# Quantised feed-forward stage: scaled values written as unsigned integers, z quantised on GpSimd

## The reference

```python
def _affine_quantize(x):
    amin, amax = (jnp.min(x), jnp.max(x))
    scale = jnp.maximum((amax - amin) / 255.0, 1e-08)
    zp = jnp.clip(jnp.round(-amin / scale) + QMIN, QMIN, QMAX)
    q = jnp.clip(jnp.round(x / scale) + zp, QMIN, QMAX)
    return (q, scale, zp)
def _qlinear(x, W, b):
    xq, sx, zx = _affine_quantize(x)
    wq, sw = _sym_quantize(W)
    acc = jnp.einsum('bsh,oh->bso', xq - zx, wq)
    return acc * (sx * sw) + b
h = _qlinear(x, W1, b1)
h = jax.nn.gelu(h, approximate=False)
out = _qlinear(h, W2, b2)
```

## Time and profile before

| | us |
|---|---|
| median of 3 runs | 2394.42 (2391.53 to 2396.53) |
| the profiled execution | 2395.65 |
| its span, first to last instruction | 2393.8 |
| the stage that the diff touches | 1087.8 to 1231.2 of it |

### The profile page before, as it was taken

How to read it: one execution, slowest core, us unless ns; L and a number is a source line. 1 busy time by engine, 2 the same in 40 slices (tenths; PEclk the granted TensorE clock), 3 DMA queues, 4 the chain that set the end, 5 groups by cost and what they waited for, 6 DMA issues and landing times.

```text
span 2393.8 us, 49297 instructions
## 1 busy us (share of the span) xinstructions
PE 2226.8 (93%) x14668; PEld 1911.1 (80%) x14669; DVE 1855.0 (77%) x4483; ACT 1492.6 (62%) x3090; POOL 689.6 (29%) x926
## 2 busy tenths in 40 slices
PE   7899999999899999995479999999997999979999
PEld 6788888888698888872257888888886888879998
DVE  3789888888875888887975888788888666865666
ACT  5566666666444677768886666666664564636666
POOL 2255555555412122210001111111112342422334
PEclk9999999999899999996589999999999999989999
DMA  8454454445201454430034544544542000114555
GB/s 219 117 145 126 141 148 142 131 137 148 69 0 35 128 139 132 137 111 6 0 90 130 144 137 140 149 142 137 143 125 62 1 1 4 37 54 141 140 140 159
DMA packets 461647, 256.58 MB, mean 107 GB/s; under 512 B 25665, under 2 KB 442333, under 8 KB 461533
## 3 DMA queue, kind: packets, MB, share of 16 engines
q1 hardware_dynamic: 461532, 255.27, 38.1%
HBM read 150.10 MB, written 105.12 MB: 107 GB/s over the span
## 4 chain that ended last, share of the span: by engine, by line
PE 78%; DVE 11%; ACT 5%; issue 4%; POOL 0%; DVEq 0%; ACTq 0%; POOLq 0%
PE ps_o L1021 13%; PE ps_s L1008 11%; PE ps_t L993 6%; PE ps_p L87 6%; PE ps_p L89 6%; PE ps_p L88 6%; PE ps_o L1704 3%; PE ps_t L1704 2%; PE ps_t L3359 2%; PE ps_s L3341 2%; PE ps_s L87 2%; PE ps_o L3359 2%; PE ps_s L89 2%; PE ps_s L88 2%; DVE a_sm L1351 2%
## 5 line engine op out<-in xcount | busy, mean ns | idle before, releaser
L1021 PEld LDWEIGHTS ps_o<-a_val,a_pt 128*128 128x128 f32 (+2 forms) x3200 | 414.6, 192 | 40.1 <-issue 9.6
L1021 PE MATMUL ps_o<-a_val,a_pt 128*128 128x128 f32 (+2 forms) x3200 | 427.2, 276 | 5.9 <-ACT a_pt L1205 4.0
L1008 PE MATMUL ps_s<-a_keys,a_zt 128*128 128x308 f32 (+1 forms) x1024 | 415.2, 492 | 5.6 <-DVE a_e L1343 3.4
L1351 DVE TENSOR_REDUCE a_sm<-a_e 128x16 f32<-128x1232 f32 (+1 forms) x192 | 234.3, 1220 | 183.2 <-ACT a_e L1213 182.7
L1175 ACT ACTIVATE a_stage<-ps_p 128x512 f32<-128x512 f32 (+1 forms) x349 | 208.7, 598 | 251.7 <-PE ps_p L89 249.4
L1205 ACT ACTIVATE a_pt<-ps_t 128x512 f32<-128x512 f32 (+1 forms) x448 | 225.2, 505 | 144.0 <-PE ps_t L993 142.7
L993 PE MATMUL ps_t<-ident,a_e 128*128 128x128 f32 (+1 forms) x1600 | 262.9, 277 | 28.3 <-POOL a_e L1368 13.8
L1166 ACT ACTIVATE a_keys<-ps_p 128x308 f32<-128x308 f32 x566 | 241.2, 427 | 73.2 <-PE ps_p L89 73.2
L87 PE MATMUL ps_p<-ct_hi,a_mt_hi 96*128 (+1 forms) x566 | 275.0, 486 | 0.0
L1213 ACT ACTIVATE a_e<-a_e 128x1232 f32<-128x1232 f32 (+1 forms) x192 | 204.2, 1063 | 70.6 <-DVE a_e L1343 54.5
L1368 POOL TENSOR_TENSOR a_e<-a_e,a_rs 128x539 f32<-128x539 f32 (+1 forms) x192 | 165.8, 891 | 229.2 <-DVE a_rs L1356 227.7
(11 more groups left out here) (437 smaller groups left out, 5064.8 us busy)
## 6 DMA issues: line engine op xcount, KB each, us to landing
a_vals<-a_stage SPq DMA_DIRECT2D x160, 512.0 KB, 3.5
a_val<-a_vals SPq DMA_DIRECT2D x128, 576.0 KB
f_w<-in_L_ffn_W_dram SPq DMA_DIRECT2D x129, 256.0 KB, 2.7
a_vals<-a_stage SPq DMA_DIRECT2D x40, 416.0 KB
a_val<-a_vals SPq DMA_DIRECT2D x64, 256.0 KB
a_val<-a_vals SPq DMA_DIRECT2D x128, 40.0 KB
x<-in_x_dram SPq DMA_DIRECT2D x8, 512.0 KB, 6.9
out_dram<-x SPq DMA_DIRECT2D x7, 512.0 KB, 6.7
```

The source lines that it names most:

```text
L1008: mm = eng.matmul(o, self.zt[:, par, cols], self.keys[:, par, k, h0:h0 + nh, :], start=True, stop=True)
L1021: mm = eng.matmul(c.ps_o[:, (i % 2) * P:(i % 2 + 1) * P], self.pt[0:r, n, :], self.val[0:r, i % 2, n, :], start=(n == 0), stop=(n == self. ...
L1351: eng.tensor_reduce(self.sm[:, :], e, AX.X, ALU.add).then_inc(st.sem, 1)
```

## The change

The values are no longer rounded by adding MAGIC to an f32. The engine writes its result as an unsigned integer, and this conversion rounds and cuts off.

z: GpSimd scales and shifts z, four tensor_scalars of 128x128 with an 8-bit result (`z8`), and turns the group into bf16 integers less the zero point with one tensor_scalar of 128x512 (`zq`). ScalarE's shift_z and VectorE's round_z are gone. The transposes are of bf16, and ScalarE's copy out of PSUM is a plain copy.

h: ScalarE shifts all 2048 columns and writes 16-bit integers to one of two places in group 0 of h (`u16`); VectorE cuts off at 255, takes the zero point off and writes bf16 to one of two places in group 1 of h (`hq`), in one tensor_scalar of 2048 columns. Group 0 itself is shifted in two halves to the two z buffers. VectorE converts group 0 only when group 1 has been shifted, since its place lies in group 1. Of the last group VectorE takes the ranges in two halves, after the second and the fourth Gelu.

```diff
+        def shift_z(g):
+            if g >= 2:
+                eng.wait_ge(self.rounded.sem, self.rounded.at(g - 1))
+            for k in range(GT):
+                b = GT * g + k
+                eng.tensor_scalar(self.z8(g % 2)[:, k * P:(k + 1) * P], self.core.x[:, b, :],
+                                  self.row[:, 0, b:b + 1], self.row[:, 1, b:b + 1], ALU.mult, ALU.add)\
+                   .then_inc(self.shifted.sem, 1)
+        def integers_z(g):
+            if g >= 2:
+                eng.wait_ge(self.zq_turned.sem, self.zq_turned.at(g - 1))
+            eng.wait_ge(self.shifted.sem, self.shifted.at(GT * g + GT))
+            eng.tensor_scalar(self.zq(g % 2), self.z8(g % 2), 1.0, self.sc[:, 0, 6:7], ALU.mult, ALU.add)\
+               .then_inc(self.rounded.sem, 1)
...
+        for g in range(1, GROUPS):
+            shift_z(g)
+            integers_z(g)
...
-        def round_z(g, par):
-            z = self.zu(par)
-            eng.wait_ge(self.shifted.sem, self.shifted.at(GT * g + GT))
-            eng.tensor_scalar(z, z, self.LEVELS, MAGIC, ALU.min, ALU.add).then_inc(self.rounded.sem, 1)
...
-        def round_h(g):
-            h = self.h[:, ds(g, 1), :, :].rearrange("p a c t -> p (a c t)")
-            eng.wait_ge(self.h_shifted.sem, self.h_shifted.at(g + 1))
-            eng.tensor_scalar(h, h, self.LEVELS, MAGIC, ALU.min, ALU.add).then_inc(self.h_rounded.sem, 1)
...
+        def integers(g, par):
+            src, dst = [self.u16(par)], [self.hq(par)]
+            if isinstance(g, int) and g < 2:
+                eng.wait_ge(self.h_shifted.sem, self.h_shifted.at(3))
+                if g == 0:
+                    half = self.UNITS // 2
+                    src = [self.zu(n).bitcast(U16) for n in range(2)]
+                    dst = [self.hq(0)[:, n * half:(n + 1) * half] for n in range(2)]
+            else:
+                eng.wait_ge(self.h_shifted.sem, self.h_shifted.at(g + 2))
+                eng.wait_ge(self.out_done.sem, self.out_done.at(g - 1))
+            for a, b in zip(src, dst):
+                eng.tensor_scalar(b, a, self.LEVELS, self.sc[:, 1, 6:7], ALU.min, ALU.add)\
+                   .then_inc(self.hq_ready.sem, 1)
...
-                mm = eng.transpose(c.bank(5 + par)[:, k * P:(k + 1) * P], self.zu(par)[:, k * P:(k + 1) * P],
-                                   c.ident[:, :])
+                mm = eng.transpose(turned(5 + par, k), self.zq(par)[:, k * P:(k + 1) * P], c.ident_bf[:, :])
...
+            if isinstance(g, int) and g < 3:
+                eng.wait_ge(self.h_shifted.sem, self.h_shifted.at(2))
+            else:
+                eng.wait_ge(self.hq_ready.sem, self.hq_ready.at(g))
+            eng.activation(self.u16(par), self.units(g), ACT.Relu, scale=self.sc[:, 1, 1:2],
+                           bias=self.sc[:, 1, 3:4]).then_inc(self.h_shifted.sem, 1)
```

More of the change, by code:

```diff
@@ L2043, in zqt, with z8, zq, u16 @@
         return self.zqt0[:, :] if par == 0 else self.h[:, GROUPS - 1, 3, 2 * P:4 * P].bitcast(BF16)
[L2045 to L2062, removed]
+    def z8(self, par):
+        return self.zu(par)[:, 0:P].bitcast(U8)
+    def zq(self, par):
+        return self.zu(par)[:, 2 * P:4 * P].bitcast(BF16)
+    def u16(self, par):
+        return self.h[:, 0, 2 * par:2 * par + 2, :].rearrange("p c t -> p (c t)").bitcast(U16)
+    def hq(self, par):
+        return self.h[:, 1, 2 * par:2 * par + 2, :].rearrange("p c t -> p (c t)").bitcast(BF16)
+    def units(self, g):
+        return self.h[:, ds(g, 1), :, :].rearrange("p a c t -> p (a c t)")
     def load(self, eng):
@@ L2109, in late_scales @@
         do = lambda ins: self.chain.step(eng, ins)
-        do(eng.tensor_scalar(sc(6), sc(3), -1.0, MAGIC, ALU.mult, ALU.subtract))
+        do(eng.tensor_scalar(sc(6), sc(3), -1.0, None, ALU.mult))
         do(eng.tensor_tensor(sc(4), sc(0), self.ws[:, 0, n:n + 1], ALU.mult))
@@ L2197, in vector @@
         eng.sem_inc(self.bias_ready.sem, 1)
-        def round_h(g):
-            h = self.h[:, ds(g, 1), :, :].rearrange("p a c t -> p (a c t)")
-            eng.wait_ge(self.h_shifted.sem, self.h_shifted.at(g + 1))
-            eng.tensor_scalar(h, h, self.LEVELS, MAGIC, ALU.min, ALU.add).then_inc(self.h_rounded.sem, 1)
[L2204 to L2214, removed]
+        def integers(g, par):
[12 more added lines that the diff above has]
+                   .then_inc(self.hq_ready.sem, 1)
+        integers(0, 0)
         def step(g, par, left):
@@ L2283, in tensor, with output @@
         eng.wait_ge(self.bias_ready.sem, self.bias_ready.at(1))
-        def output(g, par, first=False):
+        def output(g, par):
             o = c.bank(7 - 3 * par)
@@ L2288, in output @@
             eng.matmul(o, self.ones[:, :], self.bias_rows[:, :].unsqueeze(1).broadcast_to([P, GT, P]), start=True, stop=False)
-            eng.wait_ge(self.low_ready.sem, self.low_ready.at(g + 1))
-            eng.wait_ge(self.high_ready.sem, self.high_ready.at(g + 1))
-            hq = [self.hq(g, par, first, half) for half in range(2)]
+            eng.wait_ge(self.hq_ready.sem, self.hq_ready.at(g + 2))
             for k in range(GT):
                 for j in range(C):
-                    at = (j % 2) * GT * P + k * P
-                    mm = eng.matmul(o[:, k * P:(k + 1) * P], hq[j // 2][:, at:at + P], self.wt[:, 1, j, :],
+                    at = j * GT * P + k * P
+                    mm = eng.matmul(o[:, k * P:(k + 1) * P], self.hq(par)[:, at:at + P], self.wt[:, 1, j, :],
                                     start=False, stop=(k == GT - 1 and j == C - 1))
             mm.then_inc(self.out_done.sem, 1)
-        output(0, 0, True)
+        output(0, 0)
         output(1, 1)
@@ L2313, in scalar @@
                .then_inc(self.wt_ready.sem, 1)
-        def shift_z(g, par):
-            if not (isinstance(g, int) and g < 2):
-                eng.wait_ge(self.zq_turned.sem, self.zq_turned.at(g - 1))
-            for k in range(GT):
-                b = GT * g + k
-                eng.activation(self.zu(par)[:, k * P:(k + 1) * P], c.x[:, ds(b, 1), :].rearrange("p a d -> p (a d)"),
-                               ACT.Relu, scale=self.row[:, 0, ds(b, 1)], bias=self.row[:, 1, ds(b, 1)])\
-                   .then_inc(self.shifted.sem, 1)
         def copy_z(g, par):
             eng.wait_ge(self.zq_turned.sem, self.zq_turned.at(g + 1))
-            eng.activation(self.zqt(par), c.bank(5 + par), ACT.Identity, bias=self.sc[:, 0, 6:7])\
+            eng.activation(self.zqt(par), c.bank(5 + par)[:, 0:GT * P // 2].bitcast(BF16), ACT.Copy)\
                .then_inc(self.zqt_ready.sem, 1)
@@ L2354, in scalar, with shift_h @@
         eng.wait_ge(self.scale_ready.sem, self.scale_ready.at(2))
[L2356 to L2373 removed]
+        def shift_h(g, par):
+            if isinstance(g, int) and g == 0:
+                half = self.UNITS // 2
+                for n in range(2):
+                    eng.activation(self.zu(n).bitcast(U16), self.units(0)[:, n * half:(n + 1) * half], ACT.Relu,
+                                   scale=self.sc[:, 1, 1:2], bias=self.sc[:, 1, 3:4]).then_inc(self.h_shifted.sem, 1)
+                return
+            if isinstance(g, int) and g < 3:
+                eng.wait_ge(self.h_shifted.sem, self.h_shifted.at(2))
+            else:
+                eng.wait_ge(self.hq_ready.sem, self.hq_ready.at(g))
+            eng.activation(self.u16(par), self.units(g), ACT.Relu, scale=self.sc[:, 1, 1:2],
+                           bias=self.sc[:, 1, 3:4]).then_inc(self.h_shifted.sem, 1)
+        shift_h(0, 0)
+        shift_h(1, 1)
+        shift_h(2, 0)
         def step(g, par, left):
[L2376 to L2377 removed]
             if left > 2:
[L2379 removed]
+                shift_h(g + 3, 1 - par)
         for_groups(eng, step, peel=2)
```

87 lines of the change are left out of this document (32 added, 55 removed).

## The result

| | before | after |
|---|---|---|
| median, us | 2394.89 | 2376.84 |
| lowest to highest | 2391.53 to 2396.53 | 2374.06 to 2378.39 |
| profiled execution, time and span | 2395.65, 2393.8 | 2378.39, 2376.5 |

The ratio is 0.9921, 95% interval 0.9903 to 0.9939: 18.1 us faster. A further execution, 3779.49 us at a mean clock of 0.577, was disturbed and is left out.

What follows compares the result with a forecast made beforehand. VectorE was taken to bound the first sweep and ScalarE the second; +4.2 us (GpSimd then setting sweep one) and -11.5 us make -7.3, so 2394.4 - 7.3 = 2387.1 us, range 2379 to 2400.

Steps and rivals of the forecast that it cites:

- What bounds the two sweeps before: Feed-forward stage before the change: VectorE sets the first sweep at 4.38 us per group, ScalarE the second at 2.81.
- Four cost 4 x 0.797 = 3.2 us: First sweep: GpSimd's four 128x128 tensor_scalars per group, priced at 0.797 us each from a row of another stage.
- I take u = 1.5: First sweep: u, the time of GpSimd's 128x512 tensor_scalar, taken as 1.5 us between estimates of 1.12 and 2.59.
- GpSimd becomes the engine that sets the first sweep: First sweep: GpSimd's period of 4.8 us per group exceeds VectorE's 4.38, so the sweep ends 4.2 us later.
- 16T + 13.2: First sweep's length: 16 groups at GpSimd's period T (forecast 4.8 us), then 13.2 us to the total range.
- Rival 1: First sweep: GpSimd keeps up at 4.42 us per group, VectorE sets it, -1.2 us; whole kernel 2381.7; chance 0.25.
- roughly line-rate: Skill's rule for one-input elementwise GpSimd work; prediction: casts at 0.83 ns a column agree, the 797 ns row mostly doesn't.
- Second sweep, -11.5 us: Second sweep: without its 768-column conversions ScalarE paces at 1.99 us per group; 48.9 us falls to 37.4.
- full-clock sum of 36.4: Second sweep at TensorE's full clock: twelve 1.99 us steps to shift 15's end at 33.1, then conversion, matmuls, addition: 36.4 us.
- The some 1 us: Second sweep: if VectorE's 2048-column conversion took the skill's 693 ns, not 1.23 us, head and tail shorten some 1 us.
- Rival 3: Second sweep: TensorE stays at half clock and sets it, -8.3 us; whole kernel 2390.3; chance 0.16.
- The halves gain nothing: First sweep's end: taking the last group's ranges in halves saves nothing, as VectorE is still on group 14.

Runs made afterwards that it cites:

- experiments 1 and 2: Changed kernel with its second sweep put back as before: 2391.08 us; changed kernel with its first sweep put back as before: 2382.05 us.
- experiment 4: Changed kernel plus 18 GpSimd tensor_scalars of varied operations, result types and widths behind its last group, where GpSimd idles: 2374.59 us, one execution.
- Experiments 4 to 6: Changed kernel with 18 added GpSimd probes: 2374.59 us; with subtract for add in the four small tensor_scalars: 2377.46; in the large one too: 2392.54.
- experiment 6: Changed kernel with subtract for add in GpSimd's four 128x128 and its 128x512 tensor_scalars of sweep one: 2392.54 us, ratio 0.9988.

## Why the prediction was wrong, by its steps

- **What bounds the two sweeps before**: right. VectorE set the first and ScalarE the second; giving each less to do moved its sweep (experiments 1 and 2).
- **"Four cost 4 x 0.797 = 3.2 us"**: wrong, and this is the step that failed. Measured 1.76. The row I took it from the earlier trace rows has the same instruction, shape, inputs and engine, and an f32 result for a uint8 one, which experiment 4 shows to cost nothing. But its operations are (subtract, mult), and the change's are (mult, add). A trace's row doesn't name the operations; the code of that line does, and I didn't set the two side by side. Experiments 4 to 6 show it.
- **"I take u = 1.5"**, bounds 1.12 to 2.59: wrong, 0.695, below the lower bound, since every bound had the 0.80 us in it. The slope in the lower bound (0.83 ns, from the casts) was right for (mult, add). For the operations of the row that I priced from, 1.5 would have been too small: with subtracts the large one takes 2.00 us, and the kernel lands at 2392.5, 2.5 us under the kernel before (experiment 6).
- **"GpSimd becomes the engine that sets the first sweep", +4.2 us**: wrong, because T is 2.61 and not 4.8. The structure held: with T raised to 4.65 and 5.27 the sweep took 87.5 and 97.4 us, where 16T + 13.2 gives 87.6 and 97.5.
- **Rival 1** (chance 0.25) is what happened in kind: GpSimd keeps up, VectorE sets the sweep, no waits after the first. Its -1.2 us was taken at T = 4.42; the first Gelu waits for two groups of GpSimd, so T = 2.61 takes 2 x 1.81 = 3.6 us more off: -4.8. Measured -4.6. No rival had a T below 4.42.
- **The Trainium skill's "roughly line-rate"** (GPSIMD Engine Reference, Engine selection) agrees with 0.83 ns a column for (mult, add), and not with 3.3 for the forms with a subtract. I had read the 0.80 us as speaking against the rule in general.
- **Second sweep, -11.5 us**: the mechanism right, the term too small; measured -13.2. A shift with an integer result costs as much as one with an f32 result, 2.0 us. Two sizes were off. I had put 1.0 us on for a clock between the two levels; the sweep ran at 0.99 from 1183.4 on (0.78 over the sweep before), and at 0.50 only for its head. And the conversion costs 0.75 us, not 1.23. That shortens the tail: from the end of shift 15 to the end of the last addition it is 2.7 us, not 3.3. The head gained nothing, though its conversions were cheaper (halves 0.48 for 0.745): VectorE's first addition stands ahead of conversion 2 and waits 1.46 us for the first product, which runs at half clock (1.89 us), and shift 4 waits 0.59 us for that conversion. It starts 9.07 us behind the first shift, where the sum has 7.1 + 1.99 = 9.1. So the prediction's full-clock sum of 36.4 becomes 35.7, which is what was measured. The Trainium skill (VectorE: DVE Perf Modes, The perf-mode tier table) has 693 ns for 2048 bf16 columns; the row, from uint16 to bf16, says 0.75, with the next instruction starting 0.67 later. The some 1 us that the prediction drew from it for head and tail came out as 0.7.
- **Rival 3** (TensorE at half clock sets the second sweep): out. The 16 matmuls took 1.89, then 1.38, then 1.07 us, and TensorE waits for the conversion in the steady part.
- **"The halves gain nothing"**: the trace agrees. The last Gelu ended at 1150.08 and VectorE came to group 15 at 1169.09, without a wait. That the bias load and the weights cost nothing: no wait in the trace speaks against it; no run tested them alone.

Together: sweep one was 8.8 us off (+4.2 for -4.6), sweep two 1.7 us. Of these 8.8 us the price of a (subtract, mult), put on the small (mult, add)s and through them on the large one, is the whole. That the time lies below the range too has the same cause: the low end was rival 1 with T = 4.42.

## What to carry to other kernels

A row's price goes with its operations too, not only with engine, shape and types: before one is carried over, set the code of the two lines side by side. Where every bound is built on one row, the range is no wider than that row is certain; give one bound that does without it. GpSimd's (mult, add) tensor_scalar is cheap enough to take a quarter of an elementwise pass from ScalarE, but its first tensor_scalar behind the partition_all_reduce came 7 us or more later, so the first groups are better left to ScalarE.

## What the runs showed of the hardware

- GpSimd, tensor_scalar with two column scalars: 0.45 us for 128 columns and 0.77 for 512 with (mult, add), 0.80 and 2.07 with (subtract, mult). (add, mult) at 128 costs 0.45, (mult, subtract) 0.80. With one column scalar, 512 columns from uint8 to bf16 cost 0.695 with (mult, add) and 2.00 with (mult, subtract). One column scalar fewer saves 0.08 us at 512 columns.
- GpSimd's first tensor_scalar behind the partition_all_reduce between the sweeps started 7.10 and 7.19 us after it in the two kernels where it was due earlier; where it was due later, 8.46 and 8.88 us after it, 0.95 and 1.37 us late. Where none was there, the next stage's first TENSOR_TENSOR had a gap of 6.84 us. A cast right behind an earlier reduction had none.
- VectorE's tensor_scalar from 16-bit integers to bf16 takes 0.75 us for 2048 columns, and 0.95 where 0.40 us of it lie beside a tensor_scalar of GpSimd; GpSimd's is not lengthened.
- ScalarE takes the same 2.0 us for 2048 columns with an f32 and with a 16-bit unsigned result (1.98 and 2.00 us from start to start).
